# Second cross-attention of a two-layer decoder: score products from float32r value and rest of one head in a 32-row tile

## The chip, the cores and the metric

The kernel runs on one NeuronCore of a Trainium2 chip. Its engines are TensorE (PE in the profile; PEld are its weight loads), VectorE (DVE), ScalarE (ACT), GpSimd (POOL) and SyncE (SP, which issues the transfers). The metric is the device time of one execution in microseconds; the median of three runs before the change is 865.1 us.

## The reference

Two post-norm decoder layers over 8 batches of 256 tokens with 256 features. Layer 0 is a gated recurrence, a cross-attention with a bias and a quantised linear step; layer 1 a self-attention with relative positions, a cross-attention with a mask, and a gated feed-forward step. The change touches the cross-attention of layer 1 alone:

```python
def _L1_xattn_ref(key, value, query, mask, Wk, bk, Wq, bq, Wv, bv, Wo, bo):
    H, EDIM, DK = 16, 256, 16
    k = (key @ Wk.T + bk).reshape(bs, n_k, H, DK).transpose(0, 2, 1, 3)
    q = (query @ Wq.T + bq).reshape(bs, n_q, H, DK).transpose(0, 2, 1, 3)
    v = (value @ Wv.T + bv).reshape(bs, n_k, H, DK).transpose(0, 2, 1, 3)
    scores = jnp.einsum('bhmd,bhnd->bhmn', q, k)
    scores = jnp.where(mask, scores, jnp.float32(-10000000000.0))
    attn = jax.nn.softmax(scores / jnp.sqrt(jnp.float32(DK)), axis=3)
    out = jnp.einsum('bhmn,bhnv->bhmv', attn, v)
    return out.transpose(0, 2, 1, 3).reshape(bs, n_q, EDIM) @ Wo.T + bo
...
x = _layernorm(x + _L1_xattn_ref(ctx_1024, ctx_1024, x, mask, ...), axis=-1)
```

## The kernel before, in words

The whole decoder is one program whose order of instructions is written out by hand for each engine; engines meet by semaphores. Batches follow each other within a stage, and the end of one stage overlaps the beginning of the next. The second cross-attention is `attention_mask` (line 1350). The projected keys of all batches lie in `c_feat` by feature (128 rows, 2 halves, 2,048 tokens); they were written during the stage before.

Each batch b is done in four quarters, n = 4b + j. In a quarter four heads are handled, one in each group of 32 rows. A head has 16 features, so a group of 32 rows holds two heads. `scores` (line 1427) multiplies the stationary `q_par` (32 rows by 128 queries) with the moving `c_feat` (32 rows by 256 keys) for each of two query tiles t and four row groups g, and writes each group's result to a PSUM bank of its own, `s_bank[g]`. `q_par` holds q twice: in the copy for parity e, the 16 rows of the other head are zero. GpSimd makes it by two multiplications with a column of ones and zeros (`x1_split_half`, line 608, called by `split_q`, line 1904).

After the scores, DVE adds the mask bias and takes the row minimum (`peaks`, line 1748, the instructions of line 1757, eight a quarter), ACT takes the exponential (line 1659, eight a quarter), TensorE transposes (`turn`, line 1444, instructions of line 1453), DVE and ACT copy the transposed tiles to SBUF (lines 1765 and 1667, two each), TensorE weighs the values (`weigh`, line 1457, instructions of line 1468) and ACT copies the sum (line 1676). The order on TensorE in each quarter is: turn 0, turn 1, `scores` of the next quarter, turn 2, turn 3, `weigh` of the quarter before. Between them stand, once per batch, the transposes of the sum back (lines 1474 and 1477), of the normalised heads (line 1566), of `x_tok` (line 1538), the projection of q of batch b+2 (line 1574, instructions of line 232) and the output projection (line 1594, instructions of line 240). `scores` waits until all peaks of the quarter before have read the banks.

On GpSimd stand per batch, in this order (lines 1964 to 1991): the mask bias of batch b+1 (`make_bias`), the norm of batch b-2 (`normalise`), `add_biases`, from batch 3 on the split of x for the feed-forward step (`split_x`, which already makes a float32r value and rest), and `split_q` of batch b+2. SP (line 1994) loads the mask and the values per batch; the load of values waits until the values two batches before have been used.

The gated feed-forward step at the end uses float32r: `gate_up` (line 1494, 512 moving columns) and `down` (line 1504, 256 moving columns). Its products are sums of value and rest.

Of the kernel before, what the change touches and what calls it, by code (L numbers as in the profile page):

```python
# [16 lines left out]
F32 = mybir.dt.float32  # L17
# [4 lines left out]
ALU = mybir.AluOpType  # L22
# [5 lines left out]
P = 128  # L28
# [23 lines left out]
COLS = ["bz0", "bz1", "bh0", "bh1", "bg0", "bg1", "x0_bq0", "x0_bq1", "x0_bk0", "x0_bk1",  # L52
        "sa_bq0", "sa_bq1", "sa_bk0", "sa_bk1", "x1_bq0", "x1_bq1", "x1_bk0", "x1_bk1",
        "rel_v_last",
        "x0_bv0", "x0_bv1", "sa_bv0", "sa_bv1", "x1_bv0", "x1_bv1"] + [f"head{i}" for i in range(8)] + ["half0", "half1"]

ROWS = ["x0_bo", "sa_bo", "x1_bo"]
WMATS = ["Wz", "Wh", "Wg", "x0_Wq", "x0_Wk", "x0_Wv", "x0_Wo", "ffn", "sa_Wq", "sa_Wk", "sa_Wv",
# [3 lines left out]
def ge(eng, sem, value):  # L62

    if isinstance(value, int) and value <= 0:
        return
    eng.wait_ge(sem, value)
# [30 lines left out]
def decoder_kernel(nc, xT, ctxT, fside, mask0, mask1, wmats, cols_d, rows_d, gb, gate_up, down,  # L97
                   ident_d, rel_k_d, rel_v_d, mix_d, consts_d, out):
    ctx = ExitStack()
    with ctx:  # L100
        def sb(name, shape, dt=F32):
            return ctx.enter_context(nc.sbuf_tensor(name, shape, dt))
# [16 lines left out]
        rw = sb("rw", [P, TT, H // FT // 2, RW, 2])  # L119
        bnd_at = nc.sbuf_base  # L120
        bnd = sb("bnd", [P, TT, H * NBAND])
        zero_cell = sb("zero_cell", [1, 1])
        W = {n: w_all_mats[:, i, :, :] for i, n in enumerate(WMATS)}
        cols = sb("cols", [P, len(COLS)])
# [3 lines left out]
        neghalf = sb("neghalf", [P, TT])  # L128
        q_heads = sb("q_heads", [P, H // FT, FT, S])
        q_full = sb("q_full", [P, FT, S])  # L130
        q_par = sb("q_par", [P, 2, 2, FT, S])
        k_two = sb("k_two", [P, 2, FT, S])
        v_two = sb("v_two", [P, 2, TT, H, VW])
        Sx = sb("Sx", [P, 2, TT, S])
        Pr = sb("Pr", [P, 2, TT, S])
# [13 lines left out]
        def col(name):  # L149
            i = COLS.index(name)  # L150
            return cols[:, i:i + 1]
# [455 lines left out]

        def x1_split_half(pool, b, e):

            pool.tensor_scalar(q_par[:, b % 2, e, :, :], q_full[:, :, :], col(f"half{e}"), None,  # L610
                               ALU.mult).then_inc(x1_q_split, 1)

        def x1_mask_bias(pool, b):
# [736 lines left out]
        def attention_mask(sa_y_mm, sa_y_steps, sa_biased, sa_kept, sa_xt_mm, sa_xt_sb, sa_r_out):  # L1350
# [54 lines left out]
            def down_bank(t, tt):  # L1405

                if t < B - 2:
# [8 lines left out]
            rows_of = [Sx[:, :, :, :].rearrange("p a t k -> p (a t) k"),  # L1416
                       Pr[:, :, :, :].rearrange("p a t k -> p (a t) k")]

            def head(j, g):

                return HP * (j // 2) + 2 * g + j % 2
# [5 lines left out]
            def scores(pe, n):  # L1427

                b, j = divmod(n, NQ)
                if j == 0 and b >= KV_EARLY - B:  # L1430
                    pe.wait_ge(kv_sb, B + b + 1)
                pe.wait_ge(q_split, FT * b + j % 2 + 1)
                ge(pe, s_max, TT * 4 * n)
                for t in range(TT):
                    for g in range(4):
                        r = slice(32 * g, 32 * (g + 1))
                        last = pe.matmul(s_bank[g][:, t * S:(t + 1) * S],  # L1437
                                         q_par[r, b % 2, j % 2, j // 2, t * P:(t + 1) * P],
                                         batch(c_feat, b)[r, j // 2, :], start=True, stop=True)
                last.then_inc(s_mm, 1)  # L1440

            def mask_pe(pe):
# [454 lines left out]
            def mask_pool(pool):  # L1897
# [6 lines left out]
                def split_q(b):  # L1904

                    pool.wait_ge(q_sb, b + 1)
                    ge(pool, s_mm, NQ * (b - 1))
                    for e in range(2):
                        x1_split_half(pool, b, e)

                def add_biases(b):

# [49 lines left out]
                        .then_inc(rstd2, 1)  # L1962

                split_q(1)
                for b in range(B):
                    if b < B - 1:
                        make_bias(b + 1)
                    if b >= 2:
                        normalise(b - 2)
                    add_biases(b)  # L1970
                    if b == 1:
                        cast_weights()
                    if 3 <= b < B - 1:
                        for i in range(2):
                            split_x(b - 3, i)
                    if b < B - 2:
                        split_q(b + 2)
                normalise(B - 2)
                for n in range(NG):
                    low(n)  # L1980
# [13 lines left out]
            def mask_sp(sp):  # L1994

                def load_values(b):

                    ge(sp, pv_mm, NQ * (b - 1))
                    x1_load_values(sp, b)

                for b in range(2, B):
                    x1_load_mask(sp, b)
                    load_values(b)
                for t in range(B):
                    sp.wait_ge(xn_ready, t + 1)
                    sp.dma_start(out[t].rearrange("(t p) f -> p t f", p=P), xn_two[t % 2][:, :, :])\
                        .then_inc(stored[t % 2], 16)
                for i in range(2):
                    sp.wait_ge(stored[i], 16 * (B // 2))
# [1076 lines left out]
def lay_out(x, ctx_1024, fside_BxSxS2_0, mask_Bx1xSxS2_ik1, mask_Bx1xSxS2_bk0, w):  # L3086
# [11 lines left out]
    for short, long in (("x0", "L0_xattn"), ("sa", "L1_attn"), ("x1", "L1_xattn")):  # L3098
        for c in "qkvo":
            mats[f"{short}_W{c}"] = mat(w[f"{long}_W{c}"])  # L3100
        for c in "qkv":
            col[f"{short}_b{c}0"], col[f"{short}_b{c}1"] = halves(w[f"{long}_b{c}"])
        row[f"{short}_bo"] = w[f"{long}_bo"]
    col["bz0"], col["bz1"] = halves(w["L0_attn_bz"].reshape(-1))
    col["bh0"], col["bh1"] = halves(w["L0_attn_bh"].reshape(-1))
    col["bg0"], col["bg1"] = halves(w["L0_attn_bg"])
# [1 line left out]
        col[f"head{i}"] = (np.arange(P) // DH == i).astype(np.float32)  # L3108
    for i in range(2):
        col[f"half{i}"] = (np.arange(P) // DH % 2 == i).astype(np.float32)  # L3110
    rel_k, rel_v = w["L1_attn_rel_k"], w["L1_attn_rel_v"]
    col["rel_v_last"] = np.tile(rel_v[-1], P // DH)
    mix = np.zeros((2, P, 2 * P), np.float32)
# [53 lines left out]
```

## Time and profile before

| | |
|---|---|
| runs | 865.67, 864.0, 865.1 us; median 865.1 |
| profiled execution | 864.66 us, span 862.6 us |
| TensorE busy | 823.0 us, 95% of the span, 6,837 matmuls |
| DVE, ACT, POOL busy | 661.6, 604.0, 405.5 us |
| chain that ended last | PE 46%, ACT 9%, DVE 7% of the span (named pieces) |
| granted clock of TensorE | 0.998 of full speed |
| score products of this stage | line 1437, 512 matmuls, 32 x 128 stationary, 256 moving columns |

The profile is of one execution. A matmul's own duration includes its way through the array, so durations of neighbours overlap, and distances between starts say more than durations. A float32 product shows as two matmuls with a weight load each, a float32r product as one. The rows of a timeline give the start, the length of a run of like instructions and, in brackets, the idle time before it with what ended it.

### The profile page before, as it was taken

To read this page: it belongs to the slowest core of one execution; us is meant where nothing else is said; L and a number is where in the kernel's file an instruction comes from. 1 tells how busy PE (TensorE), PEld (TensorE's weight loads), DVE (VectorE), ACT (ScalarE), POOL (GpSimd) and SP (SyncE) were. 2 spreads that over 40 slices of the span, in tenths; PEclk is the share of its full clock that TensorE was granted. 3 is DMA by queue.
4 is the path that set the end of the run, shared out by engine and by line. 5 is a ranking of instruction groups with operands and counts; after the bars stand their busy time and mean duration, and the time that the engine had idled before them with its cause. 6 is when DMAs were issued, how large, how long until landed. Compare 5 with 4: busy or idle time off the path is not lost.

```text
span 862.6 us, 20687 instructions
## 1 busy us (share of the span) xinstructions
PE 823.0 (95%) x6837; PEld 615.4 (71%) x6837; DVE 661.6 (77%) x2480; ACT 604.0 (70%) x1581; POOL 405.5 (47%) x431
## 2 busy tenths in 40 slices
PE   9998999999999889999999999999999999999996
PEld 7876777777767666777777777667666777676785
DVE  4988888888998858777877666664888888886677
ACT  4548877777883477787876877774888888885331
POOL 2255557755544165155354532225734555325763
PEclk9999999999999999999999999999999999999999
DMA  9434100001003288977968868854000000000011
GB/s 323 150 122 123 47 26 26 26 2 39 1 14 147 99 257 270 277 236 231 284 200 255 260 203 263 244 156 162 5 29 29 29 30 30 25 2 1 14 37 49
DMA packets 96991, 101.86 MB, mean 118 GB/s; under 512 B 26910, under 2 KB 92190, under 8 KB 96631
## 3 DMA queue, kind: packets, MB, share of 16 engines
q1 hardware_dynamic: 96324, 100.20, 36.9%
q8 instruction: 56, 0.92, 0.5%
q14 instruction: 49, 0.39, 0.2%
q10 hardware_dynamic: 562, 0.35, 0.1%
HBM read 48.70 MB, written 51.82 MB: 117 GB/s over the span
## 4 chain that ended last, share of the span: by engine, by line
PE 46%; ACT 9%; DVE 7%; issue 2%; DMA 1%; POOL 1%; SPq 0%; DVEq 0%; ACTq 0%
PE bank L1453 6%; PE bank L232 6%; PE bank L240 5%; PE bank L2130 4%; PE bank L1437 4%; ACT bias_area L2468 3%; PE bank L2116 3%; PE bank L1468 3%; PE bank L2147 2%; PE bank L1494 2%; PE bank L1504 2%; PE bank L2180 2%; PE bank L2224 2%; PE bank L2218 2%; DVE Sx L1757 1%
## 5 line engine op out<-in xcount | busy, mean ns | idle before, releaser
L232 PE MATMUL bank<-x_feat,w_all_mats 128*128 128x256 f32 x384 | 93.1, 387 | 2.0 <-ACT q_full L348 0.6
L2865 POOL TENSOR_TENSOR bnd<-bnd,consts 128x60 f32<-128x60 f32 x64 | 18.1, 304 | 142.2 <-DMA bnd<-band_scratch 142.2
L232 PEld LDWEIGHTS bank<-x_feat,w_all_mats 128*128 128x128 f32 x384 | 70.2, 190 | 14.9 <-ACT rw L2510 3.8
L2468 ACT ACTIVATE bias_area<-bias_area,mq_two 128x256 f32<-128x256 f32 x128 | 66.3, 530 | 0.0
L873 ACT ACTIVATE q_heads<-bank 128x512 f32<-128x512 f32 x64 | 37.6, 588 | 34.7 <-PE bank L689 34.7
L2644 DVE COPY q_heads<-bank 128x512 f32<-128x512 f32 x64 | 41.2, 683 | 22.7 <-PE bank L2130 22.7
L1765 DVE COPY q_heads<-bank 128x512 f32<-128x512 f32 x64 | 42.1, 684 | 19.3 <-PE bank L1453 19.2
L1659 ACT ACTIVATE Sx<-Sx,mq 128x256 f32<-128x256 f32 x128 | 54.2, 498 | 3.4 <-DVE mq L1757 3.4
L865 ACT ACTIVATE Sx<-Sx,mq 128x256 f32<-128x256 f32 x128 | 54.4, 497 | 3.0 <-DVE mq L951 3.0
L959 DVE COPY q_heads<-bank 128x512 f32<-128x512 f32 x64 | 41.8, 683 | 18.3 <-PE bank L689 18.2
L865 ACT ACTIVATE Pr<-Pr,mq 128x256 f32<-128x256 f32 x128 | 54.3, 500 | 0.9 <-DVE mq L951 0.9
L1659 ACT ACTIVATE Pr<-Pr,mq 128x256 f32<-128x256 f32 x128 | 54.3, 502 | 0.0
L2486 ACT ACTIVATE w_all_mats<-bank 108x512 f32<-108x512 f32 x32 | 19.1, 597 | 47.5 <-PE bank L2162 47.5
L1757 DVE CUSTOM_DVE_ANT_0 Sx<-bank,bias_area 128x256 f32<-128x256 f32 x128 | 46.6, 420 | 7.4 <-PE bank L1437 4.1
L1667 ACT ACTIVATE q_heads<-bank 128x512 f32<-128x512 f32 x64 | 37.6, 590 | 18.5 <-PE bank L1453 17.8
L951 DVE CUSTOM_DVE_ANT_0 Sx<-bank,bias_area 128x256 f32<-128x256 f32 x128 | 46.5, 420 | 4.7 <-PE bank L675 4.2
L240 PE MATMUL bank<-w_all_mats,aT 128*128 128x256 f32 x192 | 46.9, 387 | 1.3 <-ACT q_full L888 1.3
L2636 DVE CUSTOM_DVE_ANT_0 bias_area<-bank,dist 128x256 f32<-128x256 f32 x128 | 46.7, 420 | 1.8 <-DMA dist<-skew_scratch 1.8
L951 DVE CUSTOM_DVE_ANT_0 Pr<-bank,bias_area 128x256 f32<-128x256 f32 x128 | 46.9, 419 | 0.0
L1757 DVE CUSTOM_DVE_ANT_0 Pr<-bank,bias_area 128x256 f32<-128x256 f32 x128 | 46.5, 420 | 0.0
L1453 PE MATMUL bank<-ident,Sx 128*128 128x128 f32 x256 | 38.9, 282 | 5.6 <-ACT q_heads L1667 5.1
L1453 PEld LDWEIGHTS bank<-ident,Sx 128*128 128x128 f32 x256 | 27.2, 141 | 22.7 <-issue 10.8
(292 smaller groups left out, 2397.8 us busy)
## 6 DMA issues: line engine op xcount, KB each, us to landing
dist<-skew_scratch SPq DMA_DIRECT2D x64, 296.0 KB, 4.1
skew_scratch<-rw SPq DMA_DIRECT2D x30, 588.0 KB, 4.4
bnd<-band_scratch SPq DMA_DIRECT2D x64, 108.0 KB, 2.6
band_scratch<-bias_area SPq DMA_DIRECT2D x32, 162.0 KB, 2.6
band_scratch<-bias_area SPq DMA_DIRECT2D x32, 148.0 KB, 2.2
skew_scratch<-dist SPq DMA_DIRECT2D x4, 1024.0 KB, 7.8
context_values<-dist SPq DMA_DIRECT2D x8, 512.0 KB, 2.6
v_two<-context_values SPq DMA_DIRECT2D x8, 512.0 KB, 3.6
```

The lines of the kernel that those rows point to most:

```text
L232: last = pe.matmul(dst[:, m * S:(m + 1) * S], w[:, k, m * P:(m + 1) * P], rhs[:, k, :], start=(k == 0), stop=(k == FT - 1))
L240: last = pe.matmul(dst[:, t * D:(t + 1) * D], src[:, k, t * P:(t + 1) * P], w[:, k, :], start=(k == 0), stop=(k == FT - 1))
L865: last = act.activation(rows_of(g, t), rows_of(g, t), ACT.Exp, bias=mq[:, g, t:t + 1], scale=-1.0)
L951: dve.tensor_tensor_reduce(out=rows_of(g, t), in0=s_bank[g][:, t * S:(t + 1) * S], in1=bias_two[:, b % 2, t, :], scale=-1.0, scalar=3e38, ...
L959: dve.tensor_copy(PTq[:, 4 * (n % 2) + g, :, :], t_bank[g % 2][:, :].rearrange("p (k q) -> p k q", k=TT))\
L1453: last = pe.transpose(t_bank[g % 2][:, k * S + t * P:k * S + (t + 1) * P], rows_of(g, t)[:, k * P:(k + 1) * P], ident[:, :])
L1659: last = act.activation(rows_of(g, t), rows_of(g, t), ACT.Exp, bias=mq[:, g, t:t + 1], scale=-1.0)
L1757: dve.tensor_tensor_reduce(out=rows_of(g, t), in0=s_bank[g][:, t * S:(t + 1) * S], in1=x1_bias_two[:, b % 2, t, :], scale=-1.0, scalar=3e3 ...
L1765: dve.tensor_copy(PTq[:, 4 * (n % 2) + g, :, :], t_bank[g % 2][:, :].rearrange("p (k q) -> p k q", k=TT))\
L2468: last = act.activation(rows_of(n, g)[:, t, :], rows_of(n, g)[:, t, :], ACT.Exp, bias=mq_two[:, n % 2, g, t:t + 1], scale=-1.0, accum_out= ...
L2636: dve.tensor_tensor_reduce(out=rows_of(n, g)[:, t, :], in0=s_bank[g][:, t * S:(t + 1) * S], in1=dist_pairs[:, t, 2 * j + g // 2, :, g % 2] ...
L2644: dve.tensor_copy(PTq[:, 4 * (n % 2) + g, :, :], t_bank[g % 2][:, :].rearrange("p (k q) -> p k q", k=TT))\
```

## The change

From batch 1 on, a score product takes float32r operands. A 32-row group now holds one head: its 16 rows of value (rounded to float32r) and its 16 rows of rest, in alternating rows. So that a head's rows alternate with those of its pair, the columns of Wq and Wk and their biases are permuted on the host, and the zeroing columns for batch 0 become alternating (`pair0`, `pair1`). The product with i = 0 pairs value with value and rest with rest, that with i = 1 pairs value of q with rest of k and the other way round; both add up in the same bank.

GpSimd copies q to a float32r tile twice (`q_cells`) and subtracts to get the rest (`q_low`); it copies k twice and subtracts (`k_cells`). Six transfers within SBUF per batch move every second row to the row beside it, over the other head. Batch 0 keeps its float32 products. `q_cells` lie over `q_par`, `q_low` over `k_two`, `k_cells` over weights that are no longer used; `q_par` and `k_two` are allocated earlier for it. The wait for the keys moves from TensorE to GpSimd.

```diff
             def scores(pe, n):
 
                 b, j = divmod(n, NQ)
-                if j == 0 and b >= KV_EARLY - B:
-                    pe.wait_ge(kv_sb, B + b + 1)
-                pe.wait_ge(q_split, FT * b + j % 2 + 1)
                 ge(pe, s_max, TT * 4 * n)
+                if b == 0:
+                    pe.wait_ge(q_split, j % 2 + 1)
+                elif j == 0:
+                    pe.wait_ge(q_turned, 16 * 2 * b)
+                    pe.wait_ge(k_turned, 16 * 4 * b)
                 for t in range(TT):
-                    for g in range(4):
-                        r = slice(32 * g, 32 * (g + 1))
-                        last = pe.matmul(s_bank[g][:, t * S:(t + 1) * S],
-                                         q_par[r, b % 2, j % 2, j // 2, t * P:(t + 1) * P],
-                                         batch(c_feat, b)[r, j // 2, :], start=True, stop=True)
+                    for i in range(2 if b else 1):
+                        for g in range(4):
+                            r, q = slice(32 * g, 32 * (g + 1)), slice(t * P, (t + 1) * P)
+                            if b == 0:
+                                last = pe.matmul(s_bank[g][:, t * S:(t + 1) * S], q_par[r, 0, j % 2, j // 2, q],
+                                                 batch(c_feat, b)[r, j // 2, :], start=True, stop=True)
+                            else:
+                                last = pe.matmul(s_bank[g][:, t * S:(t + 1) * S], q_cells[b % 2][r, j % 2, j // 2, q],
+                                                 k_cells[b % 2][r, 2 * i + j % 2, j // 2, :],
+                                                 start=(i == 0), stop=(i == 1))
                 last.then_inc(s_mm, 1)
...
                     pool.wait_ge(q_sb, b + 1)
                     ge(pool, s_mm, NQ * (b - 1))
-                    for e in range(2):
-                        x1_split_half(pool, b, e)
+                    pool.tensor_copy(q_cells[b % 2][:, :, :, :],
+                                     q_full[:, :, :].unsqueeze(1).broadcast_to([P, 2, FT, S])).then_inc(q_split, 1)
+                    pool.wait_ge(q_split, FT * b + 1)
+                    ge(pool, q_turned, 16 * 2 * (b - 1))
+                    pool.tensor_tensor(q_low[:, :, :], q_full[:, :, :], q_cells[b % 2][:, 0, :, :], ALU.subtract)\
+                        .then_inc(q_split, 1)
+
+                def split_k(b):
+
+                    if b == 1:
+                        pool.wait_ge(sa_y_mm, B)
+                    pool.wait_ge(kv_sb, B + b + 1)
+                    ge(pool, s_mm, NQ * (b - 1))
+                    k = batch(c_feat, b).unsqueeze(1).broadcast_to([P, 2, FT, S])
+                    pool.tensor_copy(k_cells[b % 2][:, 0:2, :, :], k).then_inc(k_high_made, 1)
+                    pool.wait_ge(k_high_made, b)
+                    pool.tensor_tensor(k_cells[b % 2][:, 2:4, :, :], k, k_cells[b % 2][:, 0:2, :, :], ALU.subtract)\
+                        .then_inc(k_low_made, 1)
...
                 split_q(1)
+                split_k(1)
...
                     if b < B - 2:
                         split_q(b + 2)
+                        split_k(b + 2)
...
+                def turn_q(b):
+
+                    sp.wait_ge(q_split, FT * (b + 1))
+                    q, low = q_cells[b % 2][:, :, :, :].bitcast(F32), q_low[:, :, :].bitcast(F32)
+                    sp.dma_start(q[1:P:2, 0, :, :], low[0:P:2, :, :]).then_inc(q_turned, 16)
+                    sp.dma_start(q[0:P:2, 1, :, :], low[1:P:2, :, :]).then_inc(q_turned, 16)
+
+                def turn_k(b):
+
+                    sp.wait_ge(k_low_made, b)
+                    k = k_cells[b % 2][:, :, :, :].bitcast(F32)
+                    sp.dma_start(k[1:P:2, 0, :, :], k[0:P:2, 2, :, :]).then_inc(k_turned, 16)
+                    sp.dma_start(k[1:P:2, 2, :, :], k[0:P:2, 0, :, :]).then_inc(k_turned, 16)
+                    sp.dma_start(k[0:P:2, 1, :, :], k[1:P:2, 3, :, :]).then_inc(k_turned, 16)
+                    sp.dma_start(k[0:P:2, 3, :, :], k[1:P:2, 1, :, :]).then_inc(k_turned, 16)
+
+                turn_q(1)
+                turn_k(1)
                 for b in range(2, B):
                     x1_load_mask(sp, b)
                     load_values(b)
+                    turn_q(b)
+                    turn_k(b)
...
+    paired = np.arange(D).reshape(-1, 2, DH).transpose(0, 2, 1).reshape(-1)
+    for c in "qk":
+        mats[f"x1_W{c}"] = mats[f"x1_W{c}"][:, paired]
+        col[f"x1_b{c}0"], col[f"x1_b{c}1"] = halves(np.asarray(w[f"L1_xattn_b{c}"])[paired])
```

## Rows read from the trace of the kernel before

**Rows 1.** Chain that ended last, 590 to 775 us: its share by line.

```profile
by line: PE bank L1453 27.8%; PE bank L1437 18.2%; PE bank L1468 10.8%; PE bank L232 6.8%; PE bank L240 6.6%; DVE Sx L1757 6.2%; ACT Sx L1659 5.7%; ACT q_heads L1667 3.7%; PE bank L1477 3.3%; PE bank L224 2.2%; issue 2.0%; DVE Pr L1757 1.8%
```

**Rows 2.** Engines' busy time in four rounds of a batch: stretch, length, busy (instructions).

```profile
707.02:712.88 5.86, 5.86 (x58) 4.27 (x57) 4.63 (x20) 5.24 (x14) 3.94 (x3) 1.00 0.01 3
712.88:718.01 5.13, 4.81 (x53) 3.26 (x52) 4.88 (x21) 3.81 (x10) 0.00 (x0) 1.00 0.15 46
718.01:723.16 5.15, 5.15 (x58) 3.71 (x57) 4.96 (x26) 5.02 (x14) 4.42 (x5) 1.00 0.22 72
723.16:729.64 6.48, 6.48 (x61) 4.71 (x60) 4.73 (x21) 5.86 (x16) 3.03 (x4) 1.00 0.01 3
sum 22.62, PE 22.30 PEld 15.95 DVE 19.20 ACT 19.93 POOL 11.39; mean PE 5.57 PEld 3.99 DVE 4.80 ACT 4.98 POOL 2.85
```

**Rows 3.** Timeline of TensorE, at 617 us and in round B.

```profile
617.27 1.15 PE L1437 MATMUL bank<-c_feat,q_par 32*128 32x256 f32 x16
...
712.88 1.15 PE L1437 MATMUL bank<-c_feat,q_par 32*128 32x256 f32 x16
713.95 1.09 PE L1453 MATMUL bank<-ident,Pr 128*128 128x128 f32 x8
...
717.46 0.63 PE L1453 MATMUL bank<-ident,Sx 128*128 128x128 f32 x4 [0.28 <-ACT q_heads L1667]
```

**Rows 4.** Line 1437 alone in growing stretches: length, matmuls, weight loads, clock.

```profile
690.24:690.40 0.16, 0.14 (x4) 0.15 (x8) 1.00 0.00 0
690.24:690.60 0.36, 0.34 (x8) 0.34 (x12) 1.00 0.00 0
690.24:690.82 0.58, 0.56 (x12) 0.54 (x16) 1.00 0.00 0
690.24:691.03 0.79, 0.78 (x16) 0.72 (x16) 1.00 0.00 0
```

**Rows 5.** Timeline of ACT from round B into C.

```profile
714.65 0.60 ACT L1667 ACTIVATE q_heads<-bank 128x512 f32<-128x512 f32 x1 [1.32 <-PE bank L1453]
...
718.81 0.58 ACT L1681 ACTIVATE x_feat<-bank 128x512 f32<-128x512 f32 x1
...
719.79 0.60 ACT L1667 ACTIVATE q_heads<-bank 128x512 f32<-128x512 f32 x1
```

**Rows 6.** Timeline of TensorE, float32r products of the feed-forward step.

```profile
842.10 0.28 PE L1504 MATMUL bank<-glu_weight_cells,glu_low_even 128*128 128x256 f32 x1
842.22 0.28 PE L1504 MATMUL bank<-glu_weight_cells,glu_high_even 128*128 128x256 f32 x1
```

**Rows 7.** Timeline of DVE through rounds B and C.

```profile
712.55 1.29 DVE L1765 COPY q_heads<-bank 128x512 f32<-128x512 f32 x2 [0.77 <-PE bank L1453]
714.09 0.42 DVE L1757 CUSTOM_DVE_ANT_0 Sx<-bank,bias_area 128x256 f32<-128x256 f32 x1 [0.26 <-PE bank L1437]
...
719.23 0.42 DVE L1757 CUSTOM_DVE_ANT_0 Sx<-bank,bias_area 128x256 f32<-128x256 f32 x1
...
723.42 1.28 DVE L1765 COPY q_heads<-bank 128x512 f32<-128x512 f32 x2
```

**Rows 8.** GpSimd: two rows of its timeline, two lines (ns min/median/max).

```profile
604.23 3.11 POOL L610 TENSOR_SCALAR q_par<-q_full,cols 128x512 f32<-128x512 f32 x2
...
718.63 0.72 POOL L1922 TENSOR_TENSOR rstd<-ve,neghalf 128x2 f32<-128x2 f32 x1 [7.67 <-DVE ve L206]
...
L1946 POOL CAST glu_x_odd<-x_feat x4: 609/614/620, 723.2 to 825.0; 128x512 fp32r<-128x512 f32 x4
...
L1949 POOL TENSOR_TENSOR glu_x_odd<-x_feat,glu_x_odd x4: 1272/1286/1307, 723.9 to 827.6; 128x512 fp32r<-128x512 f32 x4
```

**Rows 9.** Transfers: SP's timeline, and the page's issues (KB each, us to landing).

```profile
716.11 0.34 SPq L621 DMA_DIRECT2D v_two<-context_values  x1
...
skew_scratch<-dist SPq DMA_DIRECT2D x4, 1024.0 KB, 7.8
...
v_two<-context_values SPq DMA_DIRECT2D x8, 512.0 KB, 3.6
```

More of the change, by code:

```diff
@@ L54 @@
         "rel_v_last",
-        "x0_bv0", "x0_bv1", "sa_bv0", "sa_bv1", "x1_bv0", "x1_bv1"] + [f"head{i}" for i in range(8)] + ["half0", "half1"]
+        "x0_bv0", "x0_bv1", "sa_bv0", "sa_bv1", "x1_bv0", "x1_bv1"] + [f"head{i}" for i in range(8)] + ["half0", "half1"] + ["pair0", "pair1"]
 ROWS = ["x0_bo", "sa_bo", "x1_bo"]
@@ L121, in decoder_kernel @@
         bnd = sb("bnd", [P, TT, H * NBAND])
+        q_par_at = nc.sbuf_base
+        q_par = sb("q_par", [P, 2, 2, FT, S])
+        k_two_at = nc.sbuf_base
+        k_two = sb("k_two", [P, 2, FT, S])
         zero_cell = sb("zero_cell", [1, 1])
@@ L130, in decoder_kernel @@
         q_full = sb("q_full", [P, FT, S])
-        q_par = sb("q_par", [P, 2, 2, FT, S])
-        k_two = sb("k_two", [P, 2, FT, S])
         v_two = sb("v_two", [P, 2, TT, H, VW])
@@ L608, in x1_split_half @@
         def x1_split_half(pool, b, e):
-            pool.tensor_scalar(q_par[:, b % 2, e, :, :], q_full[:, :, :], col(f"half{e}"), None,
+            pool.tensor_scalar(q_par[:, b % 2, e, :, :], q_full[:, :, :], col(f"pair{e}"), None,
                                ALU.mult).then_inc(x1_q_split, 1)
@@ L1417, in attention_mask @@
                        Pr[:, :, :, :].rearrange("p a t k -> p (a t) k")]
+            q_cells = [exact_cells(f"x1_q_cells{i}", [P, 2, FT, S], q_par_at + 4 * i * 2 * FT * S) for i in range(2)]
+            q_low = exact_cells("x1_q_low", [P, FT, S], k_two_at)
+            k_cells = [exact_cells(f"x1_k_cells{i}", [P, 4, FT, S], w_all_at + 4 * 4 * (i + 1) * FT * D) for i in range(2)]
+            q_low_made, q_turned, k_high_made, k_low_made, k_turned = (
+                s_(n) for n in ("q_low_made", "q_turned", "k_high_made", "k_low_made", "k_turned"))
             def head(j, g):
@@ L3110, in lay_out @@
         col[f"half{i}"] = (np.arange(P) // DH % 2 == i).astype(np.float32)
+        col[f"pair{i}"] = (np.arange(P) % 2 == i).astype(np.float32)
     rel_k, rel_v = w["L1_attn_rel_k"], w["L1_attn_rel_v"]
```

## The prediction

> **What bounds the kernel now.** I first read the page and the chain that ended last, to see which engine the second cross-attention hangs on. In that stage the chain lies almost wholly on TensorE: the transposes of line 1453 hold 27.8% of it, the score products of line 1437 18.2%, and lines 1468, 232 and 240 most of the rest [rows 1]. The stage runs from 595 to about 773 us and handles one batch in four rounds, each from one call of `scores` to the next. I call them A (starts at scores of a batch's quarter 0), B, C and D. The table of the four rounds shows lengths of 5.86, 5.13, 5.15 and 6.48 us, and TensorE is busy for all of A, C and D and for 4.81 us of B [rows 2]. ACT is busy for 5.02 of 5.15 us in C and DVE for 4.96: both stand right behind TensorE, and this decides how much of a saving survives. The reader should therefore see two things: a shorter score call is on the path, and two other engines are nearly full.
>
> **What ends each round.** In A and D TensorE works without a break. B has its one gap: the second transposes of the round start at 717.46 after 0.28 us of waiting for ACT's copy (line 1667) [rows 3]. That copy is the last of a row that begins with the copy at 714.65, which is 1.77 us after the score call started at 712.88 and follows it through the call (1.07 us) and the first transposes [rows 3, 5]. So B is a loop through ACT, but the score call is a part of the loop, and a shorter call shortens it as well.
>
> **The score call now.** One call has 8 products, which the trace shows as 16 matmuls in four rounds of four. The counts grow from 8 to 12 to 16 matmuls with the ends of the window at 0.36, 0.58 and 0.79 us after 690.24, so the fours are about 0.216 us apart, while the second four weight loads have begun within 0.16 us, under the first four matmuls [rows 4]. A call costs 0.107 (first load) + 4 x 0.216 + 0.10 (change from and to the 128-row form) = 1.07 us, which agrees with the distance from 712.88 to the next piece of work in [rows 3] and with 1.15 us less the overlap.
>
> **The call after.** The count stays: 8 products times two (value and rest) are 16 matmuls and 16 loads, in four rounds of four, each of 32 rows and 256 columns. What changes is the price of one. No row shows a float32r product in a 32-row tile. The nearest are the float32r products of line 1504, 128 rows by 256 columns, with their own load each: they start 0.12 us apart [rows 6]. The bounds for a four: from below 0.107 us, which is the first load of [rows 4] at work, since a load must still be made for each; from above 0.216 us, as now, if load and matmul don't overlap. I take 0.12, from the row with the same columns, type and load. The saving is 4 x (0.216 - 0.12) = 0.385 us a call. It applies to batches 1 to 7, 28 calls: 10.8 us if nothing else is late. Bounds: 28 x 4 x 0.109 = 12.2 us and nothing.
>
> The Trainium skill ("TensorE: Matmul & The Clock Gate", Part 3, "The mechanism") states that a weight load overlaps a running matmul only when its row group differs. By that rule each four would pay 0.107 for the load and 0.107 for the columns, 0.214 us, and the call would stay as long as it is. The trace speaks against it at full height, where loads and matmuls of the same rows start 0.12 us apart [rows 6], and in the tiles [rows 4] the second loads begin under the first matmuls.
>
> **What is late next.** Take round starts as zero and 0.385 off each call.
> - A: 5.86 - 0.385 = 5.47. TensorE alone.
> - B: the loop through ACT, 5.13 - 0.385 = 4.75. TensorE's own work is 4.81 - 0.385, less.
> - C: ACT's work from its copy at 714.65 to the one at 719.79 is 5.02 us without a gap but 0.12 us [rows 5]; it includes the extra copy at 718.81 of batches 3 and on. In B the first copy comes at 1.77 - 0.385 = 1.385, so C's first copy cannot come before 1.385 + 5.02 = 6.40, which is 1.66 us into C where 1.385 was wanted. From there 3.36 us of copy, exponentials, copy and transposes follow as in B (5.13 - 1.77). C takes 1.66 + 3.36 = 5.02: it saves 0.13, not 0.385.
> - DVE works from 714.09 to 724.70 through B and C without a wait of note (10.6 us) [rows 7]. Its own two copies before end at 713.84 and hold its start in B at about 0.97 us, so it ends at 11.5, which is 1.75 us into D. The last transposes before the projection need that copy and would be ready at 1.6 us. D loses about 0.25 and saves 0.13. The same wait in C hides under ACT's loop.
>
> Steady batch: 0.385 + 0.385 + 0.13 + 0.13 = 1.03 us. Batches 2 to 7 are six such (batch 2 lacks the extra ACT copy but has DVE's wait in C): 6.2 us. Batch 1 has no norm work of this stage on DVE, nor that copy: 4 x 0.385 = 1.5. Sum 7.7 us.
>
> **GpSimd.** Two multiplications (3.11 us a batch) go [rows 8]. Added: a copy of q to 1,024 elements, a subtraction of 512, a copy of k to 1,024, a subtraction of 1,024. From 0.61 us a cast of 512 and 1.29 us a subtraction of 512 [rows 8] that is 1.22 + 1.29 + 1.22 + 2.58 = 6.3 us, 3.2 more. Behind it in order stand the mask bias and the norm. GpSimd has 7.67 us of idle time before the norm at 718.63 [rows 8], so this costs nothing; without that cover the norm and then a transposition of the next batch would be late.
>
> **Transfers.** SP issues six more per batch, 128 KB each, behind the load of values, which waits for the weighing of round B and starts at 716.11 [rows 9]. The score call that needs them starts at 729.64 [rows 2], 13.5 us later, some 12.7 when the rounds are shorter. 512 KB land in 3.6 us, 1,024 KB in 7.8 [rows 9], so 512 + 768 KB take about 3.6 + 6.3 = 10 us at the slower rate. It fits by 2.7 us. The mask load queued behind them is due a round later than they are. For batch 1 there is less: the split of k is ready about 604.2 + 6.3 = 610.5 [rows 8], four transfers land some 4 us later, and the call starts at 617.27 [rows 3]. The two waits added in front of a batch's first call are then met already. The new order of columns changes data, not instructions.
>
> **Rivals.**
> 1. *Nothing is lost behind it*: if fours cost 0.107 and ACT and DVE slip their work into other gaps, 12.2 us go. 852.9. For it: ACT and DVE have 2.7 and 3.4 us idle per batch [rows 2]. Against: the gaps lie in A and D.
> 2. *The call doesn't get shorter*: loads in the way, or a price per instruction. 16 in 1.07 us are 67 ns each, and no row of this stage shows them faster for a whole call. Then 0 us: 865.1. Against: four start within 0.02 us of each other, and [rows 6].
> 3. *Slower, the transfers come late*: they decide as soon as the seven of a batch need over 12.7 us together, 1.8 us each one after the other. At 3.6 us each (the landing time of one, [rows 9]) 25 us, thus 12.5 us late in six batches: +75 - 7.7, 932. At 2.2 us each, 2.7 us late, +16 - 8: 873. For it: one queue. Against: the rate in [rows 9] is for transfers that keep their engines busy, and nothing waits between the six issues.
> 4. *Slower, the float32r tiles run one after another*: 16 x 0.12 = 1.92 us a call, 28 x 0.85 = +24, 889. Nothing in the trace shows it; the four of today start together.
>
> **How the numbers follow.** The profiled execution took 864.66 us, its span 862.6; the median is 865.1. 864.66 - 7.7 = 857.0, and from the median 857.4. My own case reaches from 855 (DVE and ACT lose half of what I fear) to 860.5 (fours of 0.16). Chances: this case 0.60; rival 1 0.13; rival 2 0.11; rivals 3 and 4 0.08 and 0.06; a small gain between the first case and none 0.02. What a measurement can tell from no change is about 0.2%, 1.7 us. Faster 0.75, same 0.11, slower 0.14. The range from 852.5 to 865.5 takes in rival 1, the first case and most of rival 2.
>
> **What would show it.** The score products of batches 1 to 7 should be 448 matmuls of float32r, fours 0.12 us apart, a call of 0.69 us instead of 1.07. Rounds of a steady batch: 5.47, 4.75, 5.02, 6.35, together 21.6 instead of 22.6. Before the transposes of C and D new waits for DVE's copies, and in C for ACT's, should appear; before the score products no wait for a transfer. GpSimd's idle time before the norm should shrink to some 4 us. I am wrong if a call stays near 1.07 us, if a batch's first call waits for its transfers, or if C and D shrink by the whole 0.385.

## The result and the profile after

The changed kernel takes 855.75 us (median of four, 853.71 to 857.39) against 865.38 us beside it. The ratio is 0.988, with a 95% interval of 0.986 to 0.990, which is 8 to 12 us less. The forecast was 857.4 us in a range from 852.5 to 865.5. The profiled execution has a span of 851.9 us, 10.7 below the one of before. Not all of that is the change: the first score call of the stage starts at 593.76 us where it started at 594.77, after instructions that are the same; why it starts earlier is not shown. From that call to the end of the span it is 9.7 us.

The stage's four rounds for the same batch as in [rows 2], the table of busy times (stretch, length, then PE, PEld, DVE, ACT, POOL with counts, clock, share of the transfers' engines, GB/s), changed kernel:

```profile
700.44:705.89 5.45, 5.45 (x58) 4.08 (x58) 4.62 (x20) 5.24 (x14) 5.37 (x4) 1.00 0.01 3
705.89:710.63 4.74, 4.42 (x53) 3.09 (x53) 4.74 (x21) 3.82 (x11) 1.19 (x1) 1.00 0.18 43
710.63:715.53 4.90, 4.90 (x57) 3.50 (x57) 4.80 (x26) 4.90 (x14) 4.13 (x5) 1.00 0.70 242
715.53:721.71 6.18, 6.18 (x62) 4.47 (x61) 4.81 (x21) 5.86 (x16) 3.29 (x5) 1.00 0.01 2
sum 21.27, PE 20.95 PEld 15.13 DVE 18.97 ACT 19.82 POOL 13.98; mean PE 5.24 PEld 3.78 DVE 4.74 ACT 4.95 POOL 3.50
```

A and B are shorter by 0.41 and 0.39, C by 0.25 and D by 0.30. In B DVE is now busy for all 4.74 us, in C ACT for all 4.90: the engines that stood behind TensorE in [rows 2] are full in these rounds.

The score call in growing stretches, as [rows 4] showed it (length, matmuls, weight loads), changed kernel:

```profile
705.88:706.05 0.17, 0.16 (x4) 0.16 (x8) 1.00 0.00 0
705.88:706.13 0.25, 0.24 (x8) 0.24 (x12) 1.00 0.00 0
705.88:706.25 0.37, 0.36 (x12) 0.36 (x16) 1.00 0.00 0
705.88:706.37 0.49, 0.48 (x16) 0.48 (x16) 1.00 0.00 0
```

Each four more matmuls take 0.12 us, where it was 0.216. Four more weight loads have begun before the four matmuls that they run under are over, as before.

GpSimd's timeline, changed kernel, which answers to [rows 8]:

```profile
699.31 1.04 POOL L1923 CAST x_q_cells<-q_full 128x1024 fp32r<-128x1024 f32 x1 [2.72 <-ACT q_full L606]
700.43 1.29 POOL L1927 TENSOR_TENSOR x_q_low<-q_full,x_q_cells 128x512 fp32r<-128x512 f32 x1
701.66 1.04 POOL L1937 CAST x_k_cells<-c_feat 128x1024 fp32r<-128x1024 f32 x1
702.78 2.39 POOL L1939 TENSOR_TENSOR x_k_cells<-c_feat,x_k_cells 128x1024 fp32r<-128x1024 f32 x1
705.14 1.94 POOL L618 TENSOR_SCALAR bias_area<-mask_b 128x512 f32<-128x512 uint8 x1
711.30 0.72 POOL L1953 TENSOR_TENSOR rstd<-ve,neghalf 128x2 f32<-128x2 f32 x1 [4.22 <-DVE ve L208]
```

The splits take 5.8 us, and the norm still waits for DVE and not for GpSimd's own work: 4.22 us of idle time are left of 7.67.

### The profile page after: what moved, and what is told of

Same layout as the page of the kernel before. It is cut to its first block, busy times and chain, and to the rows that moved or that the text cites. A ratio compares the mean times of both kernels' runs of the same rounds, so it can differ in the third digit from the quotient of the medians.

```text
span 851.9 us, 20735 instructions
## 1 busy us (share of the span) xinstructions
PE 813.0 (95%) x6837; PEld 609.6 (72%) x6837; DVE 659.6 (77%) x2480; ACT 603.5 (71%) x1581; POOL 423.7 (50%) x445
## 4 chain that ended last, share of the span: by engine, by line
PE 46%; ACT 10%; DVE 6%; issue 3%; DMA 1%; POOL 1%; SPq 0%; DVEq 0%; ACTq 0%
PE bank L1468 7%; PE bank L234 6%; PE bank L242 5%; PE bank L2183 4%; ACT bias_area L2521 3%; PE bank L2169 3%; PE bank L1483 3%; PE bank L2200 2%; PE bank L1452 2%; PE bank L1509 2%; PE bank L1519 2%; PE bank L2233 2%; PE bank L2277 2%; PE bank L2271 2%; ACT Sx L1674 2%
## 5 line engine op out<-in xcount | busy, mean ns | idle before, releaser
L242 PEld LDWEIGHTS bank<-w_all_mats,aT 128*128 128x128 f32 x192 | 34.7, 190 | 11.9 <-issue 8.1
```

The lines of the kernel that those rows point to most:

```text
L242: last = pe.matmul(dst[:, t * D:(t + 1) * D], src[:, k, t * P:(t + 1) * P], w[:, k, :], start=(k == 0), stop=(k == FT - 1))
```

## Experiments

All build on the changed kernel. The part ahead of the stage differs by up to 4 us between executions (the stage's first call starts between 593.8 and 598.1 us, after the same instructions), so a total that was taken once says little. The rounds decide: in two executions of the changed kernel they agree within 0.02 us.

**1. The added work alone.** The tiles, splits, transfers and waits stay; the two products become one of float32.

```diff
-                    for i in range(2 if b else 1):
+                    for i in range(1):
...
-                                last = pe.matmul(s_bank[g][:, t * S:(t + 1) * S], q_cells[b % 2][r, j % 2, j // 2, q],
-                                                 k_cells[b % 2][r, 2 * i + j % 2, j // 2, :],
-                                                 start=(i == 0), stop=(i == 1))
+                                last = pe.matmul(s_bank[g][:, t * S:(t + 1) * S],
+                                                 q_cells[b % 2][r, j % 2, j // 2, q].bitcast(F32),
+                                                 k_cells[b % 2][r, j % 2, j // 2, :].bitcast(F32),
+                                                 start=True, stop=True)
```

> The changed kernel with its GpSimd splits, its six transfers a batch and its waits, but with one float32 product per tile in place of the two float32r ones (so the scores of batches 1 to 7 are left without their rest and mix in the neighbour's rows: part of the computation is changed). My theory is that the splits and transfers cost nothing and the whole gain is the call: fours 0.216 us apart, call 1.07, rounds 5.85, 5.14, 5.14, 6.48 (22.6 a batch), and the time of the kernel before within 0.2%, 863.6 to 867. Rival: the added work costs something that the shorter call hides in the changed kernel: then a batch takes over 22.7 us here and the time is above 867.

Measured: 866.43 us against 866.19, ratio 1.000 (0.999 to 1.002). Its four rounds, same view:

```profile
710.31:716.16 5.85, 5.85 (x57) 4.26 (x56) 4.62 (x20) 5.24 (x14) 5.77 (x4) 1.00 0.01 3
716.16:721.31 5.15, 4.83 (x54) 3.27 (x53) 4.90 (x21) 3.83 (x11) 0.78 (x1) 1.00 0.18 33
721.31:726.45 5.14, 5.14 (x58) 3.70 (x57) 4.96 (x26) 5.01 (x14) 4.42 (x5) 1.00 0.66 234
726.45:732.93 6.48, 6.48 (x61) 4.71 (x60) 4.73 (x21) 5.86 (x16) 2.99 (x5) 1.00 0.02 4
```

These are the rounds of [rows 2]. GpSimd's extra work and the six transfers cost nothing here, and the gain comes from the product's type. From the first call to the end of the span it is 267.8 us, as in the kernel before.

**2. A still shorter call.** One float32r product in place of two.

```diff
-                    for i in range(2 if b else 1):
+                    for i in range(1):
...
-                                                 start=(i == 0), stop=(i == 1))
+                                                 start=True, stop=True)
```

> The changed kernel with the first of the two float32r products alone (value of q with value of k, rest with rest; the mixed terms are left out). Two fours less a call, 0.23 us. My theory, that C is held by ACT and D by DVE's copies: A 5.22, B 4.51, C stays at 4.90, D 6.15 to 6.25 in place of 6.18, so 20.8 to 20.9 a batch against 21.27. Rival, that C and D are TensorE's and shrink as A and B do: 4.67 and 5.95, 20.35 a batch.

Measured rounds (855.37 us, one look):

```profile
702.57:707.87 5.30, 5.30 (x49) 3.83 (x48) 4.52 (x20) 5.30 (x14) 5.22 (x4) 1.00 0.00 0
707.87:712.42 4.55, 4.32 (x45) 2.83 (x44) 4.55 (x21) 3.74 (x11) 1.34 (x1) 1.00 0.15 22
712.42:717.40 4.98, 4.59 (x49) 3.29 (x48) 4.91 (x25) 4.98 (x14) 4.01 (x5) 1.00 0.74 260
717.40:723.70 6.30, 6.19 (x54) 4.24 (x54) 4.89 (x22) 5.91 (x16) 3.43 (x5) 1.00 0.02 4
```

In batch 1, where the other engines have less to do, each of A, B and C falls by the whole 0.23 us, from 4.74 to 4.51. In a steady batch, of four times 0.23 us only 0.14 come through: 21.13 a batch. A and B shrink by 0.15 and 0.19, C and D grow by 0.08 and 0.12. TensorE is idle for 0.39 us in C, while ACT is busy for all of it. So ACT and DVE are the next bound, and the rival, by which C and D would be TensorE's, falls. Even A is not TensorE's alone any more: ACT is busy for all 5.30 us of it. I had given 20.8 to 20.9, a miss by 0.25.

**3. Load or columns.** Half of the moving columns.

```diff
-                                last = pe.matmul(s_bank[g][:, t * S:(t + 1) * S], q_cells[b % 2][r, j % 2, j // 2, q],
-                                                 k_cells[b % 2][r, 2 * i + j % 2, j // 2, :],
+                                last = pe.matmul(s_bank[g][:, t * S:t * S + P], q_cells[b % 2][r, j % 2, j // 2, q],
+                                                 k_cells[b % 2][r, 2 * i + j % 2, j // 2, 0:P],
```

> The changed kernel with 128 instead of 256 moving columns in each product (the scores of half of the keys are left out). Theory A: a four costs what its weight loads of 128 columns cost, 0.107 to 0.115 us, so the call stays at 0.67 and the batch at 21.27. Theory B: a four costs what its 256 columns cost and falls to about 0.06 us: the call is some 0.23 us shorter and the rounds are those of the kernel with one product.

Measured, call in growing stretches:

```profile
708.79:708.82 0.03, 0.02 (x4) 0.02 (x4) 1.00 0.00 0
708.79:708.89 0.10, 0.09 (x4) 0.09 (x4) 1.00 0.00 0
708.79:708.93 0.14, 0.13 (x4) 0.13 (x8) 1.00 0.00 0
708.79:709.00 0.21, 0.20 (x8) 0.20 (x8) 1.00 0.00 0
708.79:709.12 0.33, 0.32 (x12) 0.32 (x12) 1.00 0.00 0
708.79:709.24 0.45, 0.44 (x16) 0.44 (x16) 1.00 0.00 0
```

The fours stay 0.12 us apart with 128 columns, so the columns do not set the distance. A price per instruction does not either: four loads begin together, within 0.03 us, and the next four only some 0.1 us later. What is left is the length of a load of 128 columns, as in theory A. A load of fewer columns was not tried, so this is shown by exclusion only. The call did get shorter, 0.60 us in place of 0.67 (the work behind it starts at 709.40 and the call at 708.80), since its first four, which nothing overlaps, makes way for the second one earlier. A and B shrink by 0.07 and 0.08 with it, C stays and D grows by 0.08: 21.20 a batch, where I had given 21.27. Narrower products thus save 0.07 us a call once, not 0.06 for each four.

**4. The order inside the call.**

```diff
-                    for i in range(2 if b else 1):
-                        for g in range(4):
+                    for g in range(4):
+                        for i in range(2 if b else 1):
```

> The changed kernel with the two products of a row group directly after each other (loop over groups outside, over the two products inside); same products, same sums. Theory: a matmul on a group that is in use holds up those behind it, so only the second of one group and the first of the next run together: ten steps of 0.107 in place of four, call near 1.3 us, 28 x 0.6 = 17 us slower than the changed kernel, 872. Rival: the engine finds the four groups anyway; call 0.67, 855.7.

Measured: 855.27 us, 21.29 a batch. The call in growing stretches:

```profile
707.36:707.50 0.14, 0.13 (x4) 0.13 (x8) 1.00 0.00 0
...
707.36:707.74 0.38, 0.37 (x12) 0.37 (x15) 1.00 0.00 0
707.36:707.86 0.50, 0.49 (x16) 0.49 (x16) 1.00 0.00 0
```

The trace still shows four at a time, 0.12 us apart. My theory of a queue that holds up later groups finds no support. Whether the engine starts the groups out of turn, or the program is put in this order before it gets there, no run here shows.

**5 to 7. What holds C and D.** ACT's copy of the transposed x cut short; DVE's statistics moved from B to A; both.

```diff
-                    act.activation(batch(x_feat, b), m_bank[:, :].rearrange("p (f t) -> p f t", f=FT),
-                                   ACT.Copy).then_inc(xt_sb, 1)
+                    cells = 1 if b < B - 3 else S
+                    act.activation(batch(x_feat, b)[:, :, 0:cells],
+                                   m_bank[:, :].rearrange("p (f t) -> p f t", f=FT)[:, :, 0:cells],
+                                   ACT.Copy).then_inc(xt_sb, 1)
```
```diff
                             norm_begin(dve, y_steps, b - 2, y_mm, b - 1, m_bank, True, parts=(0,))
-                        if j == 1 and b >= 2:
                             norm_begin(dve, y_steps, b - 2, y_mm, b - 1, m_bank, True, parts=(1,))
```

> The changed kernel with ACT's copy of the transposed x in round B cut to one column per row for batches 0 to 4 (their later feed-forward input is left out). Theory of the prediction, that ACT's work between its first copies of B and C holds C: C falls from 4.90 to about 4.75, D stays near 6.18. Rival, that DVE's copies hold C: C stays within 0.04 of 4.90. Third possibility, that both hold it at the same time: C loses 0.02 to 0.05.

> The changed kernel with DVE's two statistics instructions (0.7 us) issued in round A, where DVE has 0.77 us idle, in place of round B; nothing is left out. Theory: D, held by DVE's second copy, falls from 6.18 to 6.08, the length of TensorE's own work; C stays at 4.90 if ACT holds it and falls to 4.74 if DVE does. Rival, that D's 0.1 us is not DVE's: D stays at 6.18.

> Both edits together: ACT's copy of the transposed x cut to one column for batches 0 to 4 (left out of the later input), DVE's statistics moved to round A. If ACT and DVE are all that holds C and D, C is 4.74 and D 6.08, a batch 21.0 in place of 21.27. Rival: something else holds C (the first copy of the round waits for TensorE's transposes): C stays above 4.85.

Rounds C and D, in turn with ACT's copy cut, with the statistics moved, and with both:

```profile
713.62:718.41 4.79, 4.79 (x58) 3.54 (x58) 4.72 (x25) 4.63 (x14) 4.02 (x5) 1.00 0.72 249
718.41:724.70 6.29, 6.29 (x61) 4.47 (x60) 4.88 (x21) 5.90 (x16) 3.42 (x5) 1.00 0.01 4
```
```profile
713.44:718.34 4.90, 4.88 (x57) 3.51 (x57) 4.53 (x22) 4.90 (x14) 4.78 (x6) 1.00 0.67 243
718.34:724.50 6.16, 6.16 (x61) 4.47 (x60) 4.78 (x21) 5.85 (x16) 2.64 (x4) 1.00 0.01 4
```
```profile
713.93:718.67 4.74, 4.74 (x57) 3.52 (x56) 4.57 (x22) 4.58 (x14) 4.63 (x6) 1.00 0.71 249
718.67:724.78 6.11, 6.11 (x61) 4.49 (x60) 4.73 (x21) 5.85 (x16) 2.80 (x4) 1.00 0.01 4
```

Relieving ACT alone takes 0.11 us from C, and D gives it back: 21.28 a batch. Relieving DVE alone changes nothing that counts, 21.26. Both together bring 0.23 us: C and D fall to 4.74 and 6.11, and the batch to 21.04. When one engine is relieved, the other still holds the place, so neither of the first two experiments alone would have shown that these engines hold C and D. Batch 2 of the changed kernel says the same with nothing left out: it has no copy of x, and its C and D are 4.79 and 6.29, those of the kernel with the copy cut. The totals, 856.4 to 856.7 us, cannot tell these kernels apart; the rounds can.

**8. When the transfers decide.** Each of the six in four parts of 16 rows.

```diff
-                    sp.dma_start(q[1:P:2, 0, :, :], low[0:P:2, :, :]).then_inc(q_turned, 16)
...
+                    for i in range(4):
+                        sp.dma_start(q[32 * i + 1:32 * i + 32:2, 0, :, :], low[32 * i:32 * i + 31:2, :, :]).then_inc(q_turned, 16)
...
```

> The changed kernel with each of the six transfers issued as four, of 16 rows each: 24 issues a batch with the same bytes and the same packets. SP takes about 0.65 us for each transfer now, and the six begin 0.4 us after the values and end 2.8 us after the last issue, some 7 us before the first call that waits for them. Theory, that the issue counts: 24 x 0.6 = 14.4 us, so they end about 5 us too late, every batch from 2 on is 4 to 6 us longer, 6 x 5 = 30 us, 886. Rival, that bytes count: no round changes, 855.7.

Measured: 904.95 us, slower than I gave. SP's timeline in the changed kernel, and then in this one (last issues before the call):

```profile
708.72 0.34 SPq L623 DMA_DIRECT2D v_two<-context_values  x1
...
712.24 0.60 SPq L2048 DMA_DIRECT2D x_k_cells<-x_k_cells  x1
```
```profile
744.22 0.34 SPq L623 DMA_DIRECT2D v_two<-context_values  x1
...
760.21 0.58 SPq L2050 DMA_DIRECT2D x_k_cells<-x_k_cells  x1
```

TensorE at the call that waits for them, then rounds A and D and the first 3.9 us of the next A, with the granted clock in the third column from the end:

```profile
762.17 1.23 PE L1452 MATMUL bank<-x_k_cells,x_q_cells 32*128 32x256 f32 x16 [4.88 <-DMA x_k_cells<-x_k_cells]
```
```profile
734.46:741.39 6.93, 6.92 (x56) 5.46 (x56) 3.87 (x18) 4.54 (x11) 1.94 (x1) 0.77 0.04 9
...
751.03:762.17 11.14, 6.26 (x61) 4.50 (x61) 5.66 (x22) 7.01 (x18) 7.87 (x7) 0.97 0.18 47
...
762.10:766.00 3.90, 3.83 (x27) 3.46 (x28) 2.46 (x15) 1.52 (x4) 1.94 (x1) 0.50 0.09 20
```

An issue takes SP about 0.6 us whether it moves 128 KB or 32 KB. The number of transfers decides: 24 take 16 us from first to last, and TensorE waits 4.88 us. The bytes don't: they are the same. I had left out two things. Batch 1 waits too (its call came 6.6 us late). And the clock falls: behind the wait at 762.17 the granted clock was 0.50, the level of 1.2 GHz, over the first 3.9 us, and behind the wait before that one round A had 0.77 in the mean and took 6.93 us in place of 5.45. From the first to the last call the stage is 212.0 us in place of 163.4; of these 48.6 us the seven waits are 35.2 and the seven longer rounds A 12.9. In the changed kernel the last of the six is issued at 712.24 and lands 4.0 us later, at 716.2, which is 5.5 us before the call at 721.71 that needs it.

**9 and 10. An order for both engines.** The norm's statistics go to round D, where DVE waits anyway, and DVE copies x in B in place of ACT.

```diff
-                        if j == 1 and b >= 3:
-                            turn_x(b - 3)
...
-                        if j == 1 and b >= 2:
+                        if j == (3 if b < B - 1 else 1) and b >= 2:
                             norm_begin(dve, y_steps, b - 2, y_mm, b - 1, m_bank, True, parts=(1,))
...
                         turned(n, 0)
-                        if j == 1 and b >= 2:
+                        if j == 1 and b >= 3:
+                            dve.wait_ge(xt_mm, b - 2)
+                            dve.tensor_copy(batch(x_feat, b - 3), m_bank[:, :].rearrange("p (f t) -> p f t", f=FT))\
+                                .then_inc(xt_sb, 1)
+                        if j == (3 if b < B - 1 else 1) and b >= 2:
                             norm_begin(dve, y_steps, b - 2, y_mm, b - 1, m_bank, True, parts=(2,))
```

> The changed kernel with nothing left out, but other orders: DVE does the norm's statistics in round D, where it waits for TensorE, in place of B (batch 7 keeps B), and DVE in place of ACT copies the transposed x in B for batches 3 to 7. ACT loses 0.5 us in B, DVE 0.4 us net. The two cut-down kernels before showed that C and D give way only when both engines are relieved (21.04 a batch against 21.27). Theory: C 4.74, D 6.1, batch 21.05, in all some 1.2 to 1.5 us below the changed kernel. Rival: the later norm delays the split and the transfers behind it on GpSimd and SP (they end about 4.5 us before their call by my sum); then round A begins late and the kernel is slower than the changed one.

> The changed kernel once more, beside the one with other orders, on the same chip: rounds 5.45, 4.74, 4.90, 6.18 and a ratio to the kernel before of about 0.988.

Measured: 857.87 us, ratio 0.990 (0.988 to 0.992); the changed kernel beside it 856.72, ratio 0.990 (0.987 to 0.993), with the same rounds as before within 0.01. Round A:

```profile
703.59:709.26 5.67, 5.64 (x57) 4.07 (x57) 4.95 (x23) 5.46 (x15) 4.87 (x6) 1.00 0.01 3
```

C fell to 4.74 and D to 6.12 as forecast, but A rose to 5.67: three small norm instructions now stood between DVE's two copies at the end of D, and TensorE's transposes at the start of A waited for the second. Batch 7, with norm and copy both in B, took 5.75, 4.74 and 5.38. No call waited for a transfer. The rival had the sign right for another reason.

**11. The same, mended.** The whole norm ahead of both copies in D; batch 7 as in the changed kernel. The lines added to run 9 for the norm (the rest is cut):

```diff
                             norm_begin(dve, y_steps, b - 2, y_mm, b - 1, m_bank, True, parts=(1,))
+                        if j == 3 and 2 <= b < B - 1:
+                            norm_begin(dve, y_steps, b - 2, y_mm, b - 1, m_bank, True, parts=(2,))
```

> As the kernel with other orders, nothing left out, with its two faults mended. There, round A was 5.67 in place of 5.45, since the last three small norm instructions stood between DVE's two copies at the end of D, and batch 7 had both the norm and the copy of x in B (5.75, 4.74, 5.38). Now the whole norm stands ahead of both copies in D, and batch 7 keeps the changed kernel's order. Theory: batches 3 to 6 at 5.45, 4.74, 4.74, 6.11 = 21.04 against 21.27, batch 2 the same, batch 7 as in the changed kernel: 1.1 to 1.2 us shorter stage (162.2 against 163.4 from first to last call), a ratio of 0.987. Rival: the copies at the end of D are late behind the norm instructions as well; A stays above 5.5 and nothing is won.

The four rounds of the same batch:

```profile
703.46:708.91 5.45, 5.45 (x57) 4.08 (x56) 4.62 (x20) 5.24 (x14) 5.26 (x7) 1.00 0.02 3
708.91:713.66 4.75, 4.43 (x55) 3.09 (x54) 4.75 (x20) 3.83 (x11) 4.59 (x5) 1.00 0.15 34
713.66:718.39 4.73, 4.73 (x58) 3.51 (x57) 4.66 (x23) 4.53 (x13) 3.55 (x2) 1.00 0.58 218
718.39:724.51 6.12, 6.12 (x63) 4.49 (x62) 5.82 (x26) 5.86 (x16) 0.52 (x1) 1.00 0.13 34
```

21.05 a batch, as forecast, and with nothing left out. Batches 2 to 6 gain 1.0 us together. But round A of batch 7 took 5.93 in place of 5.45, since the shorter D before it (5.23, no projection of q) gives DVE no room for the norm; TensorE waits there for DVE's copy:

```profile
745.70 1.23 PE L1468 MATMUL bank<-ident,Pr 128*128 128x128 f32 x8 [0.28 <-DVE q_heads L1780]
...
792.53 0.66 PE L226 MATMUL bank<-ident,x_tok 128*128 128x128 f32 x4 [0.39 <-POOL x_tok L1963]
```

From first to last call it is 162.85 us against 163.36: half a microsecond won of the 1.1 expected. Of this, 0.36 us go again behind the last call, where TensorE waits 0.39 us for GpSimd's normalised x in the feed-forward step; the changed kernel has no such wait there. From the first call to the end of the span the two differ by 0.15 us (258.00 against 258.15). The time, 856.47 us, ratio 0.988 (0.986 to 0.990), is that of the changed kernel for all that can be measured. It was not shown to beat it.

## Why the prediction was right

- *The bound.* That the call is on the path in all four rounds held, and run 1 shows that nothing else in the change moved the time.
- *The price of a four.* A four was taken as 0.12 and measured as 0.12; the call is 0.67 where I had 0.69, so a call saves 0.40 and not 0.385. The row at full height was a good guide for the 32-row tile. The trace thus disagrees with the rule quoted from the Trainium skill ("TensorE: Matmul & The Clock Gate", Part 3): loads run under matmuls of the same groups, or the fours would be 0.214 apart. The same section also lets a load go ahead into the background weight buffer, and the trace would fit that; what happens inside the array no run here shows.
- *A and B.* 5.47 and 4.75 forecast, 5.45 and 4.74 measured. Batch 1: 1.54 forecast, 21.89 - 20.33 = 1.56 measured.
- *C.* 5.02 forecast, 4.90 measured. The mechanism was there (runs 5 to 7), but its term was too large, and DVE, which I had hidden under ACT's loop, holds C at 4.79 when ACT is relieved. I took ACT's work as the distance of its first copies less the gap in the trace. Back to back, an ACT instruction starts some 0.1 us before the end of the one ahead of it, so the distance without a gap is 4.90, not 5.02. ACT in the changed kernel:

```profile
690.15 0.58 ACT L1696 ACTIVATE x_feat<-bank 128x512 f32<-128x512 f32 x1
690.62 0.37 ACT L1691 ACTIVATE w_all_mats<-bank 128x256 f32<-128x256 f32 x1
690.89 0.60 ACT L1682 ACTIVATE q_heads<-bank 128x512 f32<-128x512 f32 x1
```

 The last starts 0.27 us after the one before it. In the kernel before, the copy of [rows 5] at 719.79 came 0.51 us after the start of the one ahead of it:

```profile
719.28 0.38 ACT L1676 ACTIVATE w_all_mats<-bank 128x256 f32<-128x256 f32 x1
```

 So 0.24 us of the distance of 5.14 were a wait, not 0.12.
- *D.* 6.35 forecast, 6.18 measured: D loses 0.10 of the call's 0.40, where I had 0.25. The 0.25 does not follow from its own figures, which give 1.75 - 1.6 = 0.15. And DVE's row from B to D is 10.4 us and not 10.6, and starts 0.88 us into B and not 0.97, both because its instructions too start before the end of the one ahead; it ends 1.61 us into D, where I had 1.75. DVE's two copies at the end of it, and the transposes of TensorE of which the second half waits for the second copy, changed kernel:

```profile
694.59 1.28 DVE L1780 COPY q_heads<-bank 128x512 f32<-128x512 f32 x2
```
```profile
695.43 1.21 PE L1468 MATMUL bank<-ident,Pr 128*128 128x128 f32 x8
```

 The eight transposes take 1.21 us. In D of the kernel before, where the copy was early enough, they took 1.04:

```profile
724.73 1.04 PE L1453 MATMUL bank<-ident,Pr 128*128 128x128 f32 x8
```

 Moving the statistics alone gave D back 0.02 us, relieving both engines 0.07. The last 0.03 (6.11 against 6.48 - 0.40) stand in batch 1 too and stay unexplained.
- *The sum.* A steady batch saves 22.62 - 21.27 = 1.35 and not 1.03 us. Six batches times 0.3 is the 2 us by which the forecast fell short: 9.7 against 7.7 from the first call on. The step was right; two of its terms, for C and D, were too dear.
- *GpSimd and transfers.* 6.3 us forecast for the splits, 5.8 measured: a cast of 1,024 took 1.04 us, not twice 0.61. For the transfers 2.7 us were to be left, and 5.5 are. I priced them by bytes, and they go by count (run 8); at the rate I named, 768 KB are 5.9 us and not 6.3. That they fit was thus right for a wrong reason, and that part is luck.
- *The rivals.* Everything comes through (12.2 us): no, 9.7. Against it I said that the gaps lie in A and D; that holds for DVE, but 1.32 of ACT's 2.69 us lie in B [rows 2]. The call stays as long: no. Late transfers: not here, but the mechanism is real. As an estimate from 5.5 us to spare and 0.63 us an issue, it starts at about fifteen issues. The tiles run one after another: no.
- *The signs.* 448 float32r matmuls, no wait for a transfer before them and 4.2 us of idle time before the norm are there as forecast. The new waits in C and D are not listed as waits, since the records of matmuls overlap; they show as longer rows of eight transposes, 1.29 us in C (at 690.03) where it was 1.09 (at 719.09), and 1.21 in D where it was 1.04.

## What to carry to other kernels

Before costing a shorter step on a full engine, follow the rows of the other engines round by round, and not their busy shares alone. Here A and B paid out the whole saving, and C, where two engines stood within 4% of TensorE, 0.25 of 0.40. D paid 0.30 although DVE was busy for only 4.73 of its 6.48 us, because it needs a copy at the end of a row that began in B. When two engines hold the same place, relieve both in one experiment, for relieving either alone leaves the batch as long as it was. And take the distance between starts in an unbroken row, not lengths and gaps, for the work of an engine.

## What the runs showed of the hardware

- A float32 product of 256 columns in four 32-row tiles takes 0.43 us (two fours of 0.216), two float32r products 0.24 us. The value-and-rest form with a head's 16 rows of each in one tile is thus 1.8 times as fast at the same number of matmuls and loads. For the whole call, with its first load and its changes of form, it is 1.07 against 0.67 us, 1.6 times.
- Fours of float32r products stay 0.12 us apart when their columns are halved, and the order within the call does not matter (21.27 and 21.29 us a batch). Four loads begin within 0.03 us and the next four some 0.1 us later.
- An issue of a transfer within SBUF of every second row took SP 0.6 us at 128 KB and at 32 KB; the issue of the values, 512 KB, took 0.34.
- A wait of 4.9 us on TensorE was followed by 3.9 us at a granted clock of 0.50.
- Of two instructions of ACT in a row, the second starts some 0.1 us before the end of the first (690.62 + 0.37 against 690.89).
